# A Mamba-style scan and a mixture of experts on one core: two lists of expert tiles, with the last routing and ten closing sums laid beside the tiles

## The reference

```python
zxbcdt = x @ Win.T                        # z, xBC, dt
xBC = silu(causal_conv4(xBC) + conv_b)    # x_ssm, B, C
h = dA_t * h + (dt_t * x_t) * B_t         # scan over 512 tokens, 4 heads of 64, 128 states
y = C_t . h + D * x_t
y = rmsnorm(y) * norm_w * silu(z) @ Wout.T
x = layernorm(x + y)
gates = sigmoid(u @ centroids.T)          # 8 experts; the top 2, divided by their sum
h = gelu(u @ W1[e] + b1[e]); outs = h @ W2[e] + b2[e]
x = layernorm(x + sum_e gates * outs)
```

## Time and profile before

| | us |
|---|---|
| median of 3 runs | 807.89 (805.18 to 808.49) |
| the profiled execution's own time | 798.2 |
| its span, first to last instruction | 796.3 |
| TensorE busy | 673.3 (85%) |
| VectorE busy | 600.1 (75%) |
| ScalarE busy | 473.8 (60%) |
| GpSimd busy | 465.2 (58%) |

### The profile page before, as it was taken

How to read it: one execution, slowest core, us unless ns; L and a number is a source line. 1 busy time by engine, 2 the same in 40 slices (tenths; PEclk the granted TensorE clock), 3 DMA queues, 4 the chain that set the end, 5 groups by cost and what they waited for, 6 DMA issues and landing times.

```text
span 796.3 us, 21108 instructions
## 1 busy us (share of the span) xinstructions
PE 673.3 (85%) x5092; PEld 548.5 (69%) x5093; DVE 600.1 (75%) x2000; ACT 473.8 (60%) x1179; POOL 465.2 (58%) x642
## 2 busy tenths in 40 slices
PE   7969999999999999999984079999999999999200
PEld 6846666666666566666663069999999999999100
DVE  4388989998999999899974446677766667677485
ACT  3747777677677677677661045555555555555165
POOL 4023377777777777777777715555555555555464
PEclk9999999999999999999997579999999999999755
DMA  9160010111110111110100212222222222222496
GB/s 260 32 240 14 16 41 18 41 32 34 42 41 19 38 31 39 42 33 26 38 18 31 73 46 69 64 62 65 65 66 66 61 63 66 66 66 61 132 302 200
DMA packets 74802, 54.09 MB, mean 68 GB/s; under 512 B 9436, under 2 KB 70111, under 8 KB 74481
## 3 DMA queue, kind: packets, MB, share of 16 engines
q1 hardware_dynamic: 56400, 31.90, 15.3%
q0 software_dynamic: 8448, 16.93, 6.4%
q10 hardware_dynamic: 9888, 4.49, 2.0%
HBM read 31.11 MB, written 22.69 MB: 68 GB/s over the span
## 4 chain that ended last, share of the span: by engine, by line
PE 69%; DVE 9%; issue 8%; POOL 5%; ACT 4%; DMA 3%; DVEq 1%; SPq 0%; ACTq 0%; POOLq 0%
PE pl L637 16%; PE p L649 15%; PE pj L402 4%; PE p L589 4%; PE p L597 3%; POOL sorted_rows L1382 3%; PE p L551 2%; PE pj L631 2%; PE p L545 2%; ACT pair L816 2%; PE pj L410 2%; PE p L499 2%; PE p L527 2%; PE p L410 2%; PE pl L446 2%
## 5 line engine op out<-in xcount | busy, mean ns | idle before, releaser
L1450 POOL DMA_INDIRECT moe_rows<-yv,xs x136 | 147.3, 1083 | 139.4 <-DVE yv L1221 122.0
L856 ACT ACTIVATE L<-pl,b_sb 128x128 f32<-128x128 f32 x544 | 154.9, 368 | 118.8 <-PE pl L637 118.8
L637 PE MATMUL pl<-Btok,M 128*128 128x128 f32 x1088 | 151.8, 283 | 0.9 <-DVE M L1209 0.3
L1382 POOL DMA_INDIRECT sorted_rows<-pair,slot x128 | 128.3, 1002 | 35.2 <-issue 33.6
L929 DVE SCALAR_TENSOR_TENSOR acc<-pj,conv_w_sb,acc 128x511 f32<-128x511 f32 (+2 forms) x192 | 142.5, 742 | 4.0 <-ACT acc L734 1.1
L649 PE MATMUL p<-w,L 128*128 x1088 | 143.9, 275 | 1.6 <-ACT L L856 1.6
L637 PEld LDWEIGHTS pl<-Btok,M 128*128 128x128 f32 x1088 | 133.4, 193 | 5.1 <-DVE M L1209 2.7
L649 PEld LDWEIGHTS p<-w,L 128*128 128x128 f32 x1088 | 132.4, 192 | 2.0 <-issue 2.0
L1205 DVE COPY Btok<-pj 128x128 f32<-128x128 f32 x136 | 39.7, 292 | 76.5 <-PE pl L637 66.8
L734 ACT ACTIVATE acc<-pj,conv_b_sb,conv_w_sb 128x512 f32<-128x512 f32 x64 | 49.5, 773 | 33.1 <-PE pj L402 33.1
L402 PE MATMUL pj<-xT,w_xbc 128*128 128x512 f32 x128 | 66.7, 603 | 0.0
(11 more groups left out here) (203 smaller groups left out, 1328.4 us busy)
## 6 DMA issues: line engine op xcount, KB each, us to landing
xs<-sorted_rows SPq DMA_DIRECT2D x136, 65.0 KB, 1.8
xres<-in_x SPq DMA_DIRECT2D x16, 256.0 KB, 3.0
w<-in_w SPq DMA_DIRECT2D x2, 2048.0 KB, 10.3
acc<-moe_rows SPq DMA_DIRECT2D x16, 256.0 KB, 4.1
xc<-moe_rows SPq DMA_DIRECT2D x16, 256.0 KB, 5.1
out<-sz ACTq DMA_DIRECT2D x16, 256.0 KB, 5.1
moe_rows<-yv,xs POOLq DMA_INDIRECT x136, 2.4
sorted_rows<-pair,slot POOLq DMA_INDIRECT x128, 2.4
```

Of the source, the lines that this page charges most:

```text
L637: mm = pe.matmul(pl[k % 2][:, f * P:(f + 1) * P], w1e[k % 2][:, f * P:(f + 1) * P], sT[k % 2][:, :], start=True, stop=True)
L856: act.activation(hT[k % 2][:, f, :], pl[k % 2][:, f * P:(f + 1) * P], ACT.Gelu, bias=b1[:, bass.ds(e * FB + f, 1)]).then_inc(hT_ready, 1)
L1382: pool.indirect_dma_start(out=sorted_rows[:, :], out_offset=bass.IndirectOffsetOnAxis(slot[q.par][:, c, k:k + 1], 0), in_=(rowA, rowB)[k][ ...
L1450: pool.indirect_dma_start(out=moe_rows[:, :], out_offset=bass.IndirectOffsetOnAxis(xs[k][:, P:P + 1].bitcast(I32), 0), in_=ye[k % 4], in_o ...
```

## The change

**Two lists.** There are 135 tiles, none of them listed beyond what 16 sequences can need. The first list is made in the last scan slot (slot 15) on VectorE, from the counts of the first ten sequences (`EARLY`): it names 72 tiles (`FULL`) that are full of rows of these sequences. The second, of 63 tiles, is made beside tiles 4 to 40: the full tiles left over from the ten sequences, and then the rest. `found` holds a list with one tile in each partition; SP writes it to DRAM (`table_away`) and reads it back into one partition (`table_back`). Each engine waits for the list before it reads a tile's number (`table_known`).

**No slot 16.** Its work, the routing of sequence 15, and the placing of 14 and 15 stand among tiles 0 to 56, at tile numbers written out by hand. Tiles 0 and 1 are transposed and fetched within slot 15, and `up` of tile 0 stands there too. The tile buffers lie in `xT`, which is free by then, instead of in buffers of the scan.

**Ten sums beside tiles.** All rows of the first ten sequences lie in the first 88 tiles (`COVER`). From tile 94 (`FIN_AT`) a sequence begins every four tiles: VectorE's add in the first, its statistics (and `fnb` of the sequence before) in the second, moments and variance in the third; GpSimd's share of the add in the first and the root in the fourth; ScalarE's scaling eight tiles after the add, in two halves of two instructions each. Eight of the ten are sent out among the tiles. Six sequences are left for the end.

**All tiles are written out**, on all engines; there are no hardware loops any more.

```diff
-TILES = 2 * TOKENS // P + E
+TILES = 2 * TOKENS // P + E - 1
+EARLY = 10
+FULL = 72
+COVER = 88
+LATE = TILES - FULL
+SEGS = 2 * E
...
+FIN_TILES = 4
+FIN_AT = COVER + 6
...
+        w1e = [xT[:, i, :] for i in range(2)]
+        hT = [xT[:, 2 + i, :].rearrange("p (f s) -> p f s", f=FB) for i in range(2)]
+        sT = [xT[:, 4, i * P:(i + 1) * P] for i in range(2)]
         b2e = [b2e_mem[:, i, :] for i in range(4)]
-        ye = [yv[i // 2][:, i % 2, :] for i in range(4)]
+        ye = [xT[:, 5, i * P:(i + 1) * P] for i in range(4)]
...
-            for k in range(-1, SEQS + 1):
+            for k in range(-1, SEQS):
                 slot_fn(Seq(0, k), 0 <= k < SEQS, k < SEQS - 1, k > 0)
+
+        def table_known(eng, j):
+
+            eng.wait_ge(table_in, 16 if j < FULL else 32)
+
+        def expert_of(eng, j):
+
+            table_known(eng, j)
+            return eng.value_load(table[0:1, 2 * j + 1:2 * j + 2], min_val=0, max_val=E - 1)
...
+            for k in range(1, SEQS):
+                slot_dma(Seq(0, k), True, k < SEQS - 1, True)
+
+            def table_away(k, lo, hi):
+                dq.wait_ge(found_ready, k + 1)
+                dq.dma_start(tile_list[lo:hi, :], found[k][0:hi - lo, :]).then_inc(table_out, 16)
+
+            def table_back(k, lo, hi):
+                dq.wait_ge(table_out, 16 * (k + 1))
+                dq.dma_start(table[0:1, 2 * lo:2 * hi],
+                             tile_list[lo:hi, :].rearrange("j k -> (j k)").unsqueeze(0)).then_inc(table_in, 16)
+
+            def load_rows(j):
+                k = j % RING
+                table_known(dq, j)
+                wait(dq, rows_out[k], 16 * (j // RING))
+                at = dq.value_load(table[0:1, 2 * j:2 * j + 1], min_val=0, max_val=SPARE + (E - 2) * P)
...
+            table_away(0, 0, FULL)
+            table_back(0, 0, FULL)
+            for i in range(2):
+                for k in range(2):
+                    dq.wait_ge(scattered[i][k], 16 * NC * EARLY // 2)
+            for j in range(TILES):
+                if j == 46:
+                    write_pads(dq, range(E))
+                if j == 56:
+                    table_away(1, FULL, TILES)
+                if j == 60:
+                    table_back(1, FULL, TILES)
+                if j == FULL:
+                    dq.wait_ge(pads_in, 16 * E)
+                    dq.wait_ge(spare_in, 16 * E)
+                    for i in range(2):
+                        for k in range(2):
+                            dq.wait_ge(scattered[i][k], 16 * NC * SEQS // 2)
+                load_rows(j)
+                if j == COVER + RING:
+                    for k in range(RING):
+                        dq.wait_ge(rows_out[k], 16 * COVER // RING)
+                if j > COVER + RING and (j - COVER - RING - 1) % FIN_TILES == 0:
+                    load_moe((j - COVER - RING - 1) // FIN_TILES)
+
+            for k in range(RING):
...
+                pe.wait_ge(xs_in[j % RING], 16 * (j // RING + 1))
+                wait(pe, fetched, j - 1)
...
+            def up(j):
+                pe.wait_ge(w1e_ready, j + 1)
+                wait(pe, hT_ready, FB * (j - 1))
...
+            def down(j):
+                e = expert_of(pe, j)
+                pe.wait_ge(hT_ready, FB * (j + 1))
...
+                if not project:
+                    transpose_rows(0)
+                    transpose_rows(1)
...
+            pe.wait_ge(state_ready, (NC - 1) * SEQS)
+            pe.wait_ge(ms_ready, SEQS)
+            for j in range(TILES):
+                if j == 10:
+                    turn_rows(last)
+                if j == 14:
+                    logits(last)
+                if j == 24:
+                    ranks(last)
+                if j + 2 < TILES:
+                    transpose_rows(j + 2)
+                if j + 1 < TILES:
+                    up(j + 1)
+                down(j)
...
+            last = Seq(0, SEQS - 1)
+            sent = (TILES - 3 - FIN_AT - 8) // FIN_TILES + 1
+            for j in range(TILES):
+                if 4 <= j < 4 + NC:
+                    normalise(last, j - 4)
+                if j == 12:
+                    keep_turned(last)
+                if j == 13:
+                    second_rows(last)
+                if j == 16:
+                    exp_logits(last)
+                n, step = divmod(j - FIN_AT - 8, FIN_TILES)
+                if 0 <= n < sent and step < 2:
+                    finish(n, step)
+                if 0 <= n < sent and step == 2:
+                    send(n)
+                gelu(j)
+
...
+            def count_rows(seqs):
+                dve.wait_ge(rank_read, seqs)
+                in_table(dve.tensor_tensor(counts[:, 0, :], next_row[:, :], region[:, :], ALU.subtract))
...
+            def count_tiles(out):
+
+                in_table(dve.tensor_scalar(counts[:, 1, :], counts[:, 0, :], float(P - 1), None, ALU.add))
+                in_table(dve.tensor_copy(counts_i[:, :, :], counts[:, :, :]))
+                in_table(dve.tensor_scalar(counts_i[:, :, :], counts_i[:, :, :], P.bit_length() - 1, None,
+                                           ALU.logical_shift_right))
+                in_table(dve.tensor_copy(out, counts_i[:, :, :]))
+
+            def tiles_ahead(n, m):
+
+                in_table(dve.tensor_tensor(q_ahead[:, 0:n, 0:m], ahead_of[:, 0:n, 0:m],
+                                           q_tiles[:, 0:m].unsqueeze(1).broadcast_to([P, n, m]), ALU.mult))
+                in_table(dve.tensor_reduce(ends[:, 0:n], q_ahead[:, 0:n, 0:m], AX_X, ALU.add))
...
+            def find_tiles(k, n):
+
+                in_table(dve.scalar_tensor_tensor(out=steps[:, 0:n], in0=ends[:, 0:n], scalar=tile_no[:, 0:1],
+                                                  in1=steps[:, 0:n], op0=ALU.is_le, op1=ALU.mult))
+                in_table(dve.tensor_reduce(packed[:, :], steps[:, 0:n], AX_X, ALU.add))
+                in_table(dve.tensor_tensor(packed[:, :], packed[:, :], tile_row[:, :], ALU.add))
+                in_table(dve.tensor_copy(packed_i[:, :], packed[:, :]))
+                dve.tensor_scalar(found[k][:, 0:1], packed_i[:, :], 5, None, ALU.logical_shift_right)
+                dve.tensor_scalar(found[k][:, 1:2], packed_i[:, :], E - 1, None,
+                                  ALU.bitwise_and).then_inc(found_ready, 1)
+
+            def early_table(part):
+                full = starts[:, 0, :]
+                if part == 0:
+                    count_tiles(starts[:, 0:2, :])
+                    in_table(dve.tensor_copy(q_tiles[:, 0:E], full))
+                    tiles_ahead(E, E)
+                    return
+                in_table(dve.scalar_tensor_tensor(out=jump[:, 1:E + 1], in0=ends[:, 0:E], scalar=-float(P),
+                                                  in1=seg_row[:, 0:E], op0=ALU.mult, op1=ALU.add))
+                row_steps(E)
+                find_tiles(0, E)
...
+            def late_counts():
+                count_rows(SEQS)
+                count_tiles(tiles[:, :, :])
+                in_table(dve.tensor_tensor(q_tiles[:, E:SEGS], tiles[:, 1, :], starts[:, 1, :], ALU.subtract))
...
+            def fetch(j):
+                e = expert_of(dve, j)
+                wait(dve, h_psum, j - 1)
+                dve.wait_ge(sT_psum, j + 1)
+                dve.tensor_copy(sT[j % 2], pj[j % 2][:, 0:P]).then_inc(fetched, 1)
...
+                        if s.n - 2 == EARLY - 1:
+                            count_rows(EARLY)
+                    if not project and c < 2:
+                        early_table(c)
...
+                if not project:
+                    dve.wait_ge(moe_w_in, 16 * MOE_W_LOADS)
+                    dve.wait_ge(z_psum, CC * SEQS)
+                    fetch(0)
+                    fetch(1)
...
+            for j in range(TILES):
+                if j == 0:
+                    statistics(last)
+                if j == 1:
+                    take_ranks(Seq(0, SEQS - 2))
+                if j == 2:
+                    shift_rows(last)
+                if j == 4:
+                    late_starts()
+                if j == 18:
+                    gate_values(last)
+                if j == 19:
+                    gate_tops(last)
+                if j == 20:
+                    gate_places(last)
+                if j == 21:
+                    gate_picks(last)
+                if j == 26:
+                    take_ranks(last)
+                if j == 27:
+                    dve.wait_ge(rank_read, SEQS)
+                    dve.tensor_copy(pad_at[:, :], next_row[:, :]).then_inc(pads_known, 1)
+                if j == 30:
+                    late_counts()
+                if j == 33:
+                    tiles_ahead(SEGS + 1, SEGS)
+                if j == 36:
+                    late_jumps()
+                if j == 38:
+                    row_steps(SEGS + 1)
+                if j == 40:
+                    find_tiles(1, SEGS + 1)
+                n, step = divmod(j - FIN_AT, FIN_TILES)
```

(30 more changed lines are left out.)

519 lines of the change are left out of this document (232 added, 287 removed).

## The result

The kernel after takes 800.64 us (median; 795.97 to 806.71) against 804.69 us (802.33 to 808.49) for the kernel before on the same chip: ratio 0.9946, 95% interval 0.9928 to 0.9963. A gain of 4 us; 45 were forecast, and 800.6 lies far outside 751 to 784. The profiled execution of the kernel after took 801.24 us, its span is 799.4.

What follows compares the result with a forecast made beforehand. Tiles were taken as bound by TensorE and VectorE together. Terms -36.9 - 2.0 - 10.8 + 2 + 9 - 25.0 + 18 = -45.7 us, subtracted from the 807.9 median, gave about 763 us; range 751 to 784.

Steps and rivals of the forecast that it cites:

- new waits: Semaphore waits added in each tile (list, fetched, hT_ready): satisfied long before; +2 us in all, up to 6.
- GpSimd's scatters: Beside the early tiles: 16 scatters of 1.0 us, one every third tile, fit beside each tile's store; no cost added.
- GpSimd holding VectorE up: Rival, tile stage: elementwise GpSimd work beside tiles slows or blocks VectorE's operations, 12 us, time 775; chance 0.14.
- Handoff: Between scan and tiles: list made early, row load 0 at about 420, fetch 3 near 433.0 instead of 469.86; -36.9 us.
- late handoff: Rival, between scan and tiles: list transfers take 4.1 us each and TensorE's clock falls; gain there 30, time 770; chance 0.14.
- Pads: SP's queue beside tiles: eight pad writes pass, with eight tiles of ring before anyone waits for a row load; no cost added.
- Routing and list: Beside tiles 1 to 40: routing of the last sequences and second list cost +9 us, from 4 to 14.
- Loops: Tile stage: all tiles written out, period 1.942 us, 254.4 instead of 265.2 us from fetch 3 on; -10.8 us.
- One tile fewer: Tile stage: one tile less to process; -2.0 us.
- Ten sums: Ten closing sums moved beside tiles 94 to 133: -25.0 us at the end, +18 beside tiles (1.8 each).
- the sign of a wrong step: Trace of the sums beside tiles: VectorE waiting on a moe_rows transfer would show the forecast wrong.
- the forecast of the period: Tiles from 94 on, with sums beside them: period near 1.95 + 0.45 = 2.4 us.

Runs made afterwards that it cites:

- e14: The kernel after, unchanged, on a chip where the kernel before takes 797.2 us: 770.0 us, ratio 0.9663.
- e8: The kernel after, unchanged, on a chip where the kernel before takes 803.7 us: 799.6 us.
- e4: e3 with 16 scatters added beside tiles 2 to 53, into a DRAM buffer nobody reads: 786.3 us, ratio to the kernel before 0.9867.
- e12: e2 once more, on a chip where the kernel before takes 800.6 us: 818.6 us, ratio 1.0207.
- e11: The kernel after, unchanged, on a chip where the kernel before takes 800.6 us: 795.8 us, ratio 0.9926.
- e13: The kernel after with a GpSimd operation of some 0.6 us between each of 16 scatters and the store behind it: 787.0 us, ratio to before 0.9811.
- e16: e15 plus e13's inserted operation and SyncE's eight pad writes issued one at a time at loads 38 to 52: 764.2 us, ratio to before 0.9581.
- e1: The kernel after with its 16 scatters beside tiles in two rows of eight, at tiles 2 and 32: 781.6 us, kernel before 796.6.
- e15: The kernel after with transposes of tiles 0 and 1 behind the sums of squares, their fetches behind the mean squares: 765.8 us, ratio to before 0.9597.
- e2: The kernel after with 12 more scatters at tiles 58 to 91, into a DRAM buffer nobody reads: 771.7 us, kernel before 796.6.
- e3: The kernel before with its tile loops written out on every engine, nothing else changed: 783.9 us, ratio 0.984.
- e6: The kernel after with all 16 closing sums behind the last tile: 803.8 us, ratio to the kernel before 0.9984.
- e5: The kernel after, unchanged, on a chip where the kernel before takes 805.0 us: 800.0 us, ratio 0.994.
- e9: e1 once more, on a chip where the kernel before takes 803.7 us: 798.5 us.
- e10: e9 with all 16 closing sums behind the last tile: 803.1 us.

## Why the prediction was wrong

Its span was worked out against the profiled execution of the kernel before, whose time was 798.2. The kernel before takes 796.6 to 797.2 us on the chips where no signal is late, 800.6 to 805.0 on the others; its profile has no wait of the late kind. So it came from a chip of the one kind and the median of 807.9 from one of the other. I took the 9.7 us between them for something that the change leaves alone. Some 3 us of it were the luck of three executions (twenty on that chip have a median of 804.7), the rest was the sign of the thing that decided. (The sum as it stands gives 762.2 from the median; 763 was put down.)

On the kind of chip that the rows were read on, the sum can be held against e14, fetch by fetch:

| stretch | before (its trace) | forecast | e14 | e14 less forecast |
|---|---|---|---|---|
| up to fetch 3 | 469.9 | 433.0 | 439.5 | +6.5 |
| fetch 3 to 58 | 112.4 | 116.7 | 124.4 | +7.8 |
| fetch 58 to 94 | 73.1 | 70.5 | 68.9 | -1.5 |
| fetch 94 to the last | 81.6 (41 periods) | 96.3 (40) | 99.4 (40) | +3.1 |
| last fetch to the end | 59.4 | 34.4 | 36.1 | +1.8 |
| span | 796.3 | 750.8 | 768.4 | +17.7 |

The forecast's entries are the terms of its sum, with the 2 us of new waits spread over the tiles. e8 on a chip of the first kind differs from e14 mainly in one row: 150.0 from fetch 3 to fetch 58, 25.6 more.

*GpSimd's scatters: the step that failed.* "GpSimd's 16 scatters of 1.0 us, one in every third tile, fit beside one store of 1.1 us in each tile of 2" was right about GpSimd's time and about the chips of e14 (0.15 us each by e4). The term was put at nothing. On the others each costs 1.9 us (e12), because TensorE's signals come late while GpSimd issues indirect transfers 0.3 us apart: 16 x 1.9 = 30 us, of which 23 to 26 show in the stretch (e11 and e8 against e14). The rival that came nearest, GpSimd holding VectorE up, had the wrong pair of engines: in the pair shown from e8 VectorE's copies keep their 0.29 and 0.42 us; it is idle, not slowed. The lock of the shared port that the page SBUF — State Buffer of the Trainium skill (SBUF: two separate sides) describes would lengthen or delay VectorE's own copies. e13 and e16 show that beside tiles, where a GpSimd operation with 256 columns stands there (0.64 us for 0.22); in the kernel after VectorE's operations from fetch 3 to 58 are only 1.6 us longer in all than usual, where this rival had 12. The trace of before could not have shown it: its stores beside tiles have mostly 0.8 to 1.0 us of idle time before them, and it takes the time of a chip of the kind where even a row of fourteen transfers makes no signal late (e1).

*Handoff: -36.9 forecast, -30.3 in e14.* The transposes of tiles 0 and 1 stand ahead of the sums of squares on TensorE. The list's round trip is 7.3 us from its sending to the first row load (416.13 to 423.45 in e14, 420.14 to 427.48 in the kernel after), not 4.2, so TensorE waits for the first rows, with the sums of squares queued behind that wait. I had put load 0 at about 420 and so the wait at nothing. The granted clock then falls from 2.4 GHz (1.00) towards 1.2 (0.50), 0.64 on average: windows of e14, then of e15 (PEclk is the third number from the end).

```profile
421.00:427.00 6.00, 1.74 (x14) 1.09 (x11) 1.27 (x5) 0.42 (x1) 3.85 (x5) 0.85 0.24 60
427.00:434.00 7.00, 7.00 (x45) 6.99 (x45) 3.68 (x25) 0.00 (x0) 2.60 (x3) 0.64 0.27 67
```

```profile
421.00:427.00 6.00, 4.07 (x33) 3.53 (x32) 3.08 (x13) 0.42 (x1) 5.50 (x6) 1.00 0.27 69
427.00:434.00 7.00, 5.72 (x50) 5.10 (x50) 5.84 (x35) 3.56 (x10) 3.23 (x5) 1.00 0.32 78
```

TensorE's timelines of the same two kernels, e14 first (L686 and L683 are the sums of squares):

```profile
425.29 0.47 PE L585 MATMUL pj<-ident,xs 128*128 128x128 f32 x1 [3.24 <-DMA xs<-sorted_rows]
...
427.05 3.57 PE L686 MATMUL p<-ones,ysq 128*128 128x96 f32 x16
```

```profile
422.31 2.02 PE L683 MATMUL p<-ones,ysq 128*128 128x96 f32 x16 [0.97 <-ACT ysq L837]
424.62 0.33 PE L585 MATMUL pj<-ident,xs 128*128 128x128 f32 x1 [0.28 <-DMA xs<-sorted_rows]
```

With the wait behind the sums the engine stays at 2.4 GHz, and fetch 3 comes at 434.19; the whole is 4.2 us faster. (In e16's trace, of an execution 3.6 us above its median, it comes at 437.69: there the list is sent out 3.3 us later.) The step was right but for this order. The late handoff was one of the rivals and gave its size (7 us) well.

*Pads.* I counted on "eight tiles of ring before anyone waits". SyncE's row of eight pad writes takes 8.5 us in e14, and at its end TensorE waits for rows (SyncE's line, then TensorE's):

```profile
527.79 8.46 SPq L358 DMA_DIRECT2D sorted_rows<-pad_tile  x8
537.08 12.79 SPq L406 DMA_DIRECT2D xs<-sorted_rows  x9
...
539.00 0.33 PE L585 MATMUL pj<-ident,xs 128*128 128x128 f32 x1 [3.08 <-DMA xs<-sorted_rows]
```

In e16, with the writes spread, the four periods from fetch 44 take 8.7 instead of 11.1 us, 2.4 less, where 6 were expected: those had been read off e2, where the same periods take 13.9. e15 has 10.3 there without that edit, so part of the 2.4 is chance.

*Routing and list.* Plain tiles at 1.915 would take 105.3 of e14's 124.4 us from fetch 3 to 58, the pads 3.4 (11.1 less four plain periods); 15.7 are left where the term had 9, and its upper end was 14. Visits with a chain of small operations are 3.6 us where 1.9 is plain, 1.7 for 1.4 us of operations, and the register load stays behind them: 0.74 us idle after `q_tiles` where 0.36 is usual.

*Loops.* -10.8 forecast, -12.7 by e3. Plain tiles at 1.915 in e14, hiccups included, 1.94 forecast. The page Runtime: NRT & Kernel Launch of the Trainium skill (Instruction fetch mechanics) has block crossings mostly hidden; by this number that is so. *One tile fewer* and *new waits*: nothing in these tiles speaks against them.

*Ten sums.* The end lost 24.2 us (e6 less e5, from the last fetch: 60.7 against 36.5), 25.0 forecast. Beside tiles the 40 periods take 19.6 us more than e6's in the kernel after (98.25 in e8 against 78.65), 22 more than e3's in e14; 18 forecast. Net 3.8 and 4.6 us measured (e5 and e6, e9 and e10), 7 forecast. Behind the missing part stand a wait that I hadn't priced, VectorE's statistics for GpSimd's share of the add, and two loads that land late, which the prediction had named as the sign of a wrong step (waits of VectorE in e14 from 633 to 732):

```profile
DVE fst L1360 <- POOL xc L1622: 6.7, 8, 1.3
...
DVE xc L1351 <- DMA xc<-moe_rows: 1.5, 1, 1.5
DVE xc L1351 <- DMA acc<-moe_rows: 1.5, 1, 1.5
```

Part of the register load does hide beneath added operations there (idle 0.15 and 0 instead of 0.36 in the rows of the result), which I had expected to stay; the forecast of the period (2.4; measured 2.46 in e8) was the sum of two errors.

So on the one kind of chip the direction and most terms held and the sum was 18 us too good: 7 of handoff, 8 beside tiles 3 to 57, 5 in and behind the sums, against 1.5 of plain tiles. On the other kind 26 us more went to signals that no term and no rival had. The gain of 0.54% stands at the edge between "faster" and "within 0.5%"; the 0.95 for faster leaned on seven terms that could not all fail. They needn't: what was put at nothing took 26 of the 45 us.

## What to carry to other kernels

When the profile and the medians of a kernel differ by over 1%, ask first where each was taken, and treat the difference as a mechanism and not as a constant. A second indirect transfer in a tile isn't paid by GpSimd's free time alone: look whether it follows the first one at once, and try it on more than one chip. An elementwise GpSimd operation set between them isn't free either: look at the lengths of VectorE's copies beside it. Put a wait for a fresh transfer behind all the work that doesn't need it, on TensorE above all, where the wait also costs its clock; and spread a row of small DMA issues when loads share their queue.
